# High parts of the gelu outputs made on ScalarE in the first MLP of a vision tower, with four activation buffers

## The reference

```
h = h + _L0_ffn_ref(_layernorm(h, axis=-1), ...)

W0 = w_fc * C0                                   # C0, C1: mixed masks of sliced sub-layers
b0 = b_fc * c0b
h = jnp.einsum('bte,he->bth', x, W0) + b0        # 192 -> 768
h = new_gelu(h)                                  # tanh form
W1 = w_proj * C1
b1 = b_proj * c1b
out = jnp.einsum('bth,eh->bte', h, W1) + b1      # 768 -> 192
```

## Time and profile before

| | us |
|---|---|
| median of three runs | 2829.3 |
| lowest and highest | 2827.83 to 2830.43 |
| the profiled execution | 2830.04 |
| its span, first to last instruction | 2828.2 |
| first MLP in it, from first normalisation to last statistics | 548.5 to 954.4 |

### The profile page before, as it was taken

The page is one execution under the profiler, slowest core; times in us unless marked ns, Lnnn a source line. Parts: engine busy times, 40 slices in busy tenths (PEclk is TensorE's granted clock), DMA queues, the critical chain, the costliest instruction groups (busy, mean ns, idle before and its releaser), DMA issues. The chain is left out here.

```text
span 2828.2 us, 82965 instructions
## 1 busy us (share of the span) xinstructions
PE 2588.6 (92%) x27416; PEld 2173.2 (77%) x27416; DVE 2378.9 (84%) x5917; ACT 1904.5 (67%) x5750; POOL 1136.9 (40%) x1288
## 2 busy tenths in 40 slices
PE   5797888699999799999999999999999999997776
PEld 5796555477777588888888888888888888885554
DVE  6955666699999688888888888888888888887998
ACT  3343444333333388888888888888888888886998
POOL 5585333222222034334333433433333344344665
PEclk9897555599999999999999999999999999997999
DMA  9461000000000133333333333333333333330111
GB/s 286 137 187 52 0 0 0 0 1 0 0 0 0 27 79 78 73 68 77 69 72 77 77 71 70 77 68 74 77 77 70 71 75 68 75 78 9 42 40 47
DMA packets 181687, 173.31 MB, mean 61 GB/s; under 512 B 19064, under 2 KB 180290, under 8 KB 181379
## 3 DMA queue, kind: packets, MB, share of 16 engines
q1 hardware_dynamic: 181634, 172.64, 25.1%
HBM read 46.68 MB, written 9.68 MB: 20 GB/s over the span
## 5 line engine op out<-in xcount | busy, mean ns | idle before, releaser
L1183 POOL TENSOR_TENSOR b_pr<-b_pr,b_rinv 128x394 f32<-128x394 f32 (+1 forms) x768 | 625.7, 841 | 1008.4 <-DVE b_rinv L1141 1008.4
L1078 ACT ACTIVATE b_pr<-b_banks,b_nmx 128x197 f32<-128x197 f32 (+1 forms) x1536 | 625.0, 423 | 28.2 <-DVE b_nmx L1135 25.6
L1049 ACT ACTIVATE b_pt<-b_bank_t 128x394 f16<-128x394 f32 (+1 forms) x768 | 337.4, 493 | 203.5 <-PE b_bank_t L1014 203.3
L1135 DVE TENSOR_REDUCE b_nmx<-b_banks 128x2 f32<-128x394 f32 (+1 forms) x768 | 397.3, 558 | 64.7 <-PE b_banks L1004 56.5
L1106 DVE TENSOR_TENSOR b_pt<-b_bank_t,b_pt 128x394 f16<-128x394 f32 (+1 forms) x768 | 395.8, 556 | 18.3 <-ACT b_pt L1049 18.2
L988 PE MATMUL b_banks<-b_xt,wqkv 128*128 128x197 f16 x3840 | 373.6, 249 | 4.5 <-DVE b_xt L1106 2.2
L1014 PE MATMUL b_bank_t<-ident,b_pr 128*128 128x128 f32 (+3 forms) x3072 | 341.8, 253 | 3.1 <-DVE b_pt L1106 3.0
L988 PEld LDWEIGHTS b_banks<-b_xt,wqkv 128*128 128x128 f16 x3840 | 320.5, 98 | 25.7 <-issue 18.8
L1004 PE MATMUL b_banks<-b_kst,b_qst 128*128 128x197 f16 (+1 forms) x3072 | 326.9, 248 | 6.8 <-ACT b_pr L1078 5.4
L1078 ACT ACTIVATION_READ_ACCUMULATOR b_pr<-b_banks,b_nmx 128x1 f32 (+1 forms) x1536 | 315.5, 205 | 0.0
L1014 PEld LDWEIGHTS b_bank_t<-ident,b_pr 128*128 128x128 f32 (+3 forms) x3072 | 282.2, 142 | 43.2 <-issue 35.4
(11 more groups left out here) (175 smaller groups left out, 4657.4 us busy)
## 6 DMA issues: line engine op xcount, KB each, us to landing
b_qst<-b_qk SPq DMA_DIRECT2D x512, 147.8 KB, 2.5
b_kst<-b_qk SPq DMA_DIRECT2D x512, 73.9 KB, 2.3
patches<-in_x SPq DMA_DIRECT2D x64, 588.0 KB, 4.4
out<-z_res SPq DMA_DIRECT2D x32, 192.0 KB
out<-z_res SPq DMA_DIRECT2D x32, 103.5 KB
h<-in_wqkv SPq DMA_DIRECT2D x2, 1152.0 KB, 7.6
h<-in_w SPq DMA_DIRECT2D x2, 576.0 KB, 8.1
h<-in_fc SPq DMA_DIRECT2D x1, 768.0 KB
```

The lines of the kernel that those rows point to most:

```text
L1049: return nc.scalar.activation(dst, src, ACT.Copy)
L1078: last = nc.scalar.activation(pr[n % 3][0:ROWS[c], c, e, :], banks[0:ROWS[c], c, e * SEQ:(e + 1) * SEQ], ACT.Exp, bias=nmx[n % 2][0:ROWS[c ...
L1135: v.reduce_max(nmx[n % 2][0:ROWS[c], c, :], banks[0:ROWS[c], c, 0:2 * SEQ].rearrange("p (e t) -> p e t", e=2), AX.X, negate=True).then_inc ...
L1183: last = nc.gpsimd.tensor_tensor(p, p, inv, ALU.mult)
```

## The change

The f16 high part of a gelu output is made by ACT in place of DVE. In ACT's program a copy (`high_hidden`) of chunk f - 1 follows the gelu of chunk f, and that of the last chunk stands at the end of the pair. It waits for its own gelu (`gelu_made`) and signals `hid_hi`. DVE's `split_hidden` loses the cast and its wait for `gelu_made`; its subtractions wait for `hid_hi` as before. There are four activation buffers in place of two, chosen by the number of the chunk over the whole stage, (2b + f) % 4, and a gelu waits for the subtraction of four chunks before. Nothing on PE, POOL or SP is changed but line numbers: in the changed kernel L803 is the copy, L758 the subtraction, L798 ACT's part of split_x.

```diff
-        act_out = [sb(f"m_act{r}", [P, PAIR]) for r in range(2)]
+        act_out = [sb(f"m_act{r}", [P, PAIR]) for r in range(4)]
...
                 def split_hidden(u, b):
                     for f in range(HC):
                         n = chunks_before(u, b) + f + 1
-                        dve.wait_ge(gelu_made, n)
-                        v.tensor_copy(hid[b][:, 0, f, :], act_out[f % 2][:]).then_inc(hid_hi, 1)
                         dve.wait_ge(hid_hi, n)
-                        v.tensor_tensor(hid[b][:, 1, f, :], act_out[f % 2][:], hid[b][:, 0, f, :], ALU.subtract)\
+                        v.tensor_tensor(hid[b][:, 1, f, :], act_out[(2 * b + f) % 4][:], hid[b][:, 0, f, :], ALU.subtract)\
                             .then_inc(hid_split, 1)
...
+                def high_hidden(u, b, f):
+                    act.wait_ge(gelu_made, chunks_before(u, b) + f + 1)
+                    nc.scalar.activation(hid[b][:, 0, f, :], act_out[(2 * b + f) % 4][:], ACT.Copy).then_inc(hid_hi, 1)
+
                 def gelu(u, b):
                     for f in range(HC):
                         n = chunks_before(u, b) + f
                         act.wait_ge(fc_made, n + 1)
-                        if f >= 2:
-                            act.wait_ge(hid_split, n - 1)
-                        else:
-                            act.wait_ge(hid_split, chunks_before(u, b))
-                        nc.scalar.activation(act_out[f % 2][:], bank_h[(2 * b + f) % 4][:, 0:PAIR], ACT.Gelu_apprx_tanh,
+                        if not (isinstance(n, int) and n < 4):
+                            act.wait_ge(hid_split, n - 3)
+                        nc.scalar.activation(act_out[(2 * b + f) % 4][:], bank_h[(2 * b + f) % 4][:, 0:PAIR], ACT.Gelu_apprx_tanh,
                                              bias=S["fc_bias"][:, f:f + 1]).then_inc(gelu_made, 1)
+                        if f >= 1:
+                            high_hidden(u, b, f - 1)
+                    high_hidden(u, b, HC - 1)
```

## The result

The changed kernel took 2809.8 us in the median of four runs (2808.3 to 2813.7) beside 2828.8 for the kernel before: a ratio of 0.9934 with a 95% interval of 0.9917 to 0.9952. In five more runs of the same kernel it was 2807.8 beside 2827.3, ratio 0.9932 (0.9919 to 0.9946). So 19 us, where the forecast was 2811.7 and 17.6 us.

A forecast was written before the change was run, and what follows sets the result against it. VectorE was taken to bound the first MLP, with TensorE waiting on it. 29 x (12.26 - 11.64) = 18.0 us saved, less 0.4 in the head, takes the median from 2829.3 to 2811.7 us; range 2808 to 2820.

The forecast's parts named there:

- The floor of the pair: First MLP, steady pairs: TensorE without waits needs 11.64 us a pair, where pairs took 12.26.
- What was the bound: First MLP: VectorE set the pace before at 12.26 us a pair; TensorE would set it after.
- The six casts as 3.1 us: VectorE, each pair: six casts leave, 3.1 us, so its work falls from 12.26 to about 9.1 us.
- The copies: ScalarE, each pair: six copies of 0.52 us; split_x from +7.6, VectorE's ends near +9.8, 1.8 us to spare.
- The upper bound of 0.617: Copy on ScalarE: most it could take, from L1316; ScalarE's work then 7.0 us a pair in place of 6.3.
- The normalisation's margin: VectorE's normalisation ahead of TensorE's transposes of the next input: at most 0.29 us to spare, expected to cost nothing.
- The rival that made the normalisation the bound: First MLP: normalisation late by 0.1 to 0.9 us past the margin, 2815 to 2829 us, chance 0.10.
- ACT's traffic beside VectorE: Normalisation: if ScalarE's SBUF traffic slowed VectorE, copies would cost 0.5 us a pair, about 2827; with gelus too, 2849.
- The table load: Rival on ScalarE: gelu and copy alternating load tables, 1.283 us each, about 3120 us; chance 0.05 shared with later normalisation.
- The loop's branch: TensorE's hardware loop over two pairs: branch costed at nothing; uncovered it would be 0.2 x 14 = 3 us.
- The head: Start of the first MLP: +0.4 us from the chain; clock taken as 0, with -3 to +7 us possible.
- The sum: Whole kernel: 18.0 us saved in 29 pairs less 0.4 us, 17.6 us, median 2811.7 us.

The follow-up runs named there:

- Without the wait six casts: Changed kernel plus six casts a pair on VectorE into a tile nobody reads, no subtraction waiting for them: 2818.1 us, ratio 0.9943 to 0.9973.
- six dead copies: Changed kernel plus one copy that nobody reads ahead of each ScalarE copy, six a pair: 2816.4 us, ratio 0.9935 to 0.9968.
- four instructions more: Changed kernel plus four TENSOR_SCALARs into a spare tile ahead of each normalisation: 2830.8 us in one run.
- copies and two buffers: Changed kernel with two activation buffers in place of four, the copies still on ScalarE: 2880.2 us, ratio 1.0169 to 1.02.
- less of down: One of three products of parts left out of the down product: in the kernel before 2822.4 us, in the changed kernel 2753.5 us.
- three dead casts: Changed kernel plus three casts a pair on VectorE into a tile nobody reads, on chunks 0, 2 and 4: 2815.7 us, ratio 0.9938 to 0.9971.
- the waited case: Changed kernel plus six unread casts a pair on VectorE, each subtraction waiting for its cast: 2832.9 us, ratio 1.0003 to 1.0022.
- two dead copies: Changed kernel plus two copies that nobody reads ahead of each ScalarE copy: 2897.5 us in one run.

## Why the prediction was right, and where it was not

**The floor of the pair.** The one place in the trace of before where TensorE ran without a wait gave 5.94 + 5.70 = 11.64 us. All 29 steady pairs after are 11.64 or 11.65: 17.9 saved there for 18.0 in the sum. This was the number that carried the forecast, and it was read, not modelled.

**What was the bound.** Shown from both sides: less work on TensorE changed nothing in a pair before (12.26) and nearly 1.8 us after.

**The six casts as 3.1 us.** Right as what they cost in the kernel before, wrong in its reading as VectorE's own work. Without the wait six casts move VectorE on by 1.6 us (6 x 0.27, 712.70 to 712.97) and leave TensorE the bound. Beside the changed kernel even less: twelve instructions take 4.52 us there, its six subtractions 4.06 (709.07 to 713.13). VectorE's part of the pair fell to 11.64 - 2.04 = 9.6 us, not to 9.1: its subtractions now wait for copies, 0.2 us each in two places of the steady pair, and the last three are stretched beside POOL.

**The copies.** 0.527 us in the median, for 0.52 taken from L619. The upper bound of 0.617 was not needed. ACT's split_x started at +7.61 as timed, and DVE's ended at +9.94 for +9.8. That the first is right to the hundredth is in part luck: the first subtraction started 0.2 us later than I had put it (+4.74) and took 0.56 in place of 0.90, so that it freed gelu 4's buffer at +5.3 all the same. The chain had 1.7 us to spare; six dead copies used 1.5 of it (split_x over at +11.46) and were still free.

**The normalisation's margin** is the step that was mis-sized: "at most 0.29 us to spare" was 0.08. What was wrong is the place of the normalisation. I had taken it from the step after 577.91: the update at +0.20, the last L110 over at +4.56. That step is one of those written out ahead of the hardware loop. In the kernel after, the two written-out steps (576.25 and 587.89) stand exactly there; in every step of the loop, from 599.54 on, the update starts at +0.33, the statistics wait 0.15 us for it, and L110 is over at +4.80 to +4.86. It is not VectorE's wait for PE that makes the difference: it waited 2.99 us ahead of the update at 576.46 and 2.04 ahead of the one at 704.66. Half of the 0.26 us could be read in the trace of before, whose loop has the same wait where the step after 577.91 has none; why the steps of the loop are later, no run here shows. First the kernel before, written out and in the loop, then the kernel after, written out (the loop's stand above, 704.66 and 708.81):

```profile
579.29 1.14 DVE L776 BATCH_NORM_STATS2 stats<-h 128x6 f32<-128x192 f32 x4
...
700.49 1.15 DVE L769 TENSOR_TENSOR h<-m_bank_y,h 128x192 f32 x4
701.80 1.14 DVE L776 BATCH_NORM_STATS2 stats<-h  x4 [0.15 <-DVE h L769]
```

```profile
576.46 1.15 DVE L767 TENSOR_TENSOR h<-m_bank_y,h 128x192 f32<-128x192 f32 x4 [2.99 <-PE m_bank_y L852]
...
580.48 0.34 DVE L110 TENSOR_SCALAR m_xn<-h,mean,rstd 69x128 f32<-69x128 f32 x1
```

The limit itself was read nearly right. With four instructions more L110 is over at +5.47 and the pair is 0.57 longer, so TensorE is not held while it is over by +4.90: 0.34 us behind the place of the written-out steps, 0.08 behind that of the loop. The forecast held with 0.08 us a pair in hand, and that this was enough was luck. The rival that made the normalisation the bound needed only this much more, and its chance of 0.10 was low for what I knew.

**ACT's traffic beside VectorE** did not slow it: L108 took 324 to 348 ns (336 in the median) over the whole stage of the kernel after, as before.

**The table load.** One on the gelu's line, as before. Behind it lie 31 alternations of gelus and split_x in the earlier trace rows (62 copies), not the 32 of the prediction.

**The loop's branch** cost nothing: even and odd pairs are alike to 0.01 us.

**The head** was put at +0.4 and came out at -0.13 (23.32 us for the first two distances, 23.45 before): +0.14 in the first, from the chain, as foreseen in sign, and -0.27 in the second, where the up product spent less time at the lower clock. Over eight of the kernels here (all but those with copies and two buffers, with dead copies or with less of down) the second distance lies between 12.96 and 14.56 us, and in each it is 6.80 more than the up product takes from its first matmul to its last, so that the clock is all that differs. It is of the size of what I allowed for it.

**The sum.** 17.9 in the steady pairs and 0.1 in the head give, rounded, the 18.1 us of the stage, for 17.6 forecast. The median moved by 19; the last microsecond is within what the second attention varies.

## What to carry to other kernels

Look in the trace for the one place where the engine you want to be the bound ran without waiting; the spacing there is the time that a change can reach, and no sum over durations is needed for it. A gain needs each part of a change that makes it: here a ring that is worth nothing alone turned a loss of 1.8% into a gain of 0.7%. And when the bound moves, recount the margins with the new engine waiting, and take the places of the instructions from the steps of the loop, not from those written out ahead of it: here they differ by 0.26 us, where 0.34 was all there was.

## What the runs showed of the hardware

Beside GpSimd, what VectorE pays can hang on one wait. Cast and subtraction in turn, without a wait that holds (each starts 0.08 us before the one ahead of it is over, 713.45 for 712.97 + 0.56): the casts take 349 to 369 ns in all 192 cases, the four instructions of add_bias 6.4 us, and a single one of them up to 4.9. With each subtraction waiting for the cast just ahead of it: casts up to 755 ns, subtractions up to 924, add_bias 3.0. Two kernels lie between: the changed one (three subtractions in a row at full speed, 1.52 us, then waits for copies; add_bias 4.3 us, where it was 3.0) and that with three dead casts (casts up to 748 ns, subtractions up to 966, add_bias 4.65 us), where nine instructions of VectorE take 5.29 us from 710.90 on and so more than the twelve of the unwaited case. What lets GpSimd in there, without a wait for a cast, no run isolates.

The Trainium skill, SBUF — State Buffer, "SBUF: two separate sides", says of the port pair that both engines use that it is an exclusive lock, which a GpSimd instruction contends for with a VectorE instruction in a two-port mode, or with one that has two SBUF inputs if the GpSimd one reads SBUF: whichever starts first holds the pair for its whole instruction and the other blocks. The durations of the waited case fit that: each stretched one is longer by some 0.3 to 0.4 us. That a row of VectorE instructions can keep GpSimd out for several microseconds, and that a wait in between lets it in, is what these two runs add; whether the lock is kept from one instruction to the next or only retaken first, they don't tell.

TensorE's matmuls got slower behind some of its longer waits. In the three kernels where it waits 2.0 to 2.4 us in most pairs (copies with two buffers, two dead copies, the kernel before with less of down), some of the up products take 6.3 to 6.5 us from the first matmul to the last and not 4.86; the two looked at above had a granted clock of 0.75. In the kernels that wait half a microsecond a pair none does behind the head. It cost nothing where VectorE sets the pair (12.26 all through), and 0.4 to 0.8 us a time, 1.5 in the last, with two dead copies.

Here it cost nothing that POOL was slower, because its result is needed two pairs later. In a kernel that waits for POOL the same removal of a wait on VectorE could lose time; no run here has such a wait.
